# A layer of chunked attention and a mixture of experts on one Trainium2 core: all places of one attention block on the common time line, drawn anew

## What is computed

```python
x = x + layernorm(attention(layernorm(x)))        # 16 heads of 32, decayed linear attention in chunks of 128 tokens
x = x + layernorm(ffn(layernorm(x)))              # shared gated FFN (1408 wide) + top 2 of 8 experts (352 wide)

# attention, per head and chunk of 128 tokens, state S carried from chunk to chunk
inter  = (q * decay_q) @ S
intra  = ((q @ k.T) * decay_mask) @ v
S      = lam**128 * S + (k * decay_k).T @ v
out    = (inter + intra) @ w_out.T + b_out

# ffn, per token
shared = (silu(x @ gate.T) * (x @ up.T)) @ down.T
probs  = softmax(x @ router.T); top 2, renormalised
y      = sum over the 2 experts of weight * expert(x) + sigmoid(x @ shared_gate.T) * shared
```

## Time and profile before

| | us |
|---|---|
| median of 3 runs (lowest, highest) | 2009.27 (2005.46, 2009.52) |
| the profiled execution: span from first to last instruction | 2000.4 |
| its own time outside the span | not shown apart; the median of the runs is 8.9 above the span |
| TensorE busy | 1895.7 |
| VectorE, ScalarE, GpSimd busy | 1083.5, 844.6, 439.6 |
| mean granted TensorE clock | 0.985 |

### The profile page before, as it was taken

How to read it: one execution, slowest core, us unless ns; L and a number is a source line. 1 busy time by engine, 2 the same in 40 slices (tenths; PEclk the granted TensorE clock), 3 DMA queues, 4 the chain that set the end, 5 groups by cost and what they waited for, 6 DMA issues and landing times.

```text
span 2000.4 us, 27565 instructions
## 1 busy us (share of the span) xinstructions
PE 1895.7 (95%) x9880; PEld 1536.0 (77%) x9880; DVE 1083.5 (54%) x2590; ACT 844.6 (42%) x1718; POOL 439.6 (22%) x438
## 2 busy tenths in 40 slices
PE   7789999999999998999999999999999999999997
PEld 5567777777777776777777778778989888998875
DVE  4556665554554553464464454433656666666566
ACT  4334443333343332333344233123556656656554
POOL 2301001001001001001000100121455555555322
PEclk9889999999999998999999999999999999999998
DMA  8978566557367356446546456786788888888597
GB/s 304 373 258 310 184 246 250 198 187 258 122 234 259 126 173 243 177 163 239 205 174 224 171 181 240 243 325 236 236 253 241 247 247 240 255 250 251 130 283 198
DMA packets 140869, 456.84 MB, mean 228 GB/s; under 512 B 17200, under 2 KB 17344, under 8 KB 123968
## 3 DMA queue, kind: packets, MB, share of 16 engines
q1 hardware_dynamic: 90720, 251.70, 35.7%
q0 software_dynamic: 49584, 203.33, 33.0%
q10 hardware_dynamic: 432, 0.07, 0.0%
HBM read 332.99 MB, written 122.04 MB: 227 GB/s over the span
## 4 chain that ended last, share of the span: by engine, by line
PE 56%; DMA 5%; DVE 5%; ACT 2%; issue 1%; POOL 1%; SPq 1%; ACTq 0%; DVEq 0%
PE banks L796 16%; PE banks L798 16%; PE banks L797 16%; DMA moe_dn_raw<-w_dn,w_index 3%; PE banks L863 2%; PE banks L989 1%; DMA ffn_w_raw<-w_ffn 1%; PE banks L877 1%; PE banks L995 1%; PE banks L883 1%; PE banks L870 1%; DMA att_w_lo<-att_w_split 1%; PE banks L829 1%; ACT moe_dn_hi L1134 0%; DVE fin_stats L1535 0%
## 5 line engine op out<-in xcount | busy, mean ns | idle before, releaser
L796 PE MATMUL banks<-xT_hi,ffn_gate_up_hi_lo 128*128 128x512 f32 x704 | 296.7, 422 | 9.8 <-DMA xT_lo<-xt_scratch 3.3
L798 PE MATMUL banks<-xT_hi,ffn_gate_up_hi_lo 128*128 128x512 f32 x704 | 276.8, 393 | 0.0
L797 PE MATMUL banks<-xT_lo,ffn_gate_up_hi_lo 128*128 128x512 f32 x704 | 276.1, 392 | 0.0
L796 PE MATMUL banks<-moe_gu_hi,moe_xT_hi 128*128 128x352 f32 x568 | 196.5, 346 | 4.2 <-DVE moe_xT_lo L1515 4.1
L1067 ACT COPY q_one_head<-qT 32x128 f32<-32x128 f32 x512 | 151.2, 295 | 89.5 <-PE banks L863 84.0
L1508 DVE TENSOR_TENSOR moe_gu_lo<-moe_gu_raw,moe_gu_hi 128x704 fp32r<-128x704 f32 x156 | 136.0, 889 | 90.4 <-ACT moe_gu_hi L1128 85.7
L798 PE MATMUL banks<-moe_gu_hi,moe_xT_lo 128*128 128x352 f32 x568 | 183.4, 323 | 0.0
L797 PE MATMUL banks<-moe_gu_lo,moe_xT_hi 128*128 128x352 f32 x568 | 182.6, 321 | 0.0
L796 PEld LDWEIGHTS banks<-xT_hi,ffn_gate_up_hi_lo 128*128 128x128 f32 x704 | 133.1, 189 | 49.2 <-issue 10.2
L797 PEld LDWEIGHTS banks<-xT_lo,ffn_gate_up_hi_lo 128*128 128x128 f32 x704 | 133.2, 189 | 33.9 <-issue 8.9
L798 PEld LDWEIGHTS banks<-xT_hi,ffn_gate_up_hi_lo 128*128 128x128 f32 x704 | 132.9, 189 | 29.0
(11 more groups left out here) (315 smaller groups left out, 4157.6 us busy)
## 6 DMA issues: line engine op xcount, KB each, us to landing
ffn_gate_up_hi_lo<-ffn_gate_up_split SPq DMA_DIRECT2D x66, 1024.0 KB, 4.8
ffn_down_hi_lo<-ffn_down_split SPq DMA_DIRECT2D x66, 512.0 KB, 3.4
att_w_hi<-att_w_split SPq DMA_DIRECT2D x112, 256.0 KB, 4.0
att_w_lo<-att_w_split SPq DMA_DIRECT2D x112, 256.0 KB, 4.8
x_normed_by_expert<-x_normed POOLq DMA_DIRECT2D x26, 771.0 KB, 16.1
ffn_w_raw<-w_ffn SPq DMA_DIRECT2D x44, 384.0 KB, 6.0
ffn_gate_up_split<-ffn_gate_up_hi_lo SPq DMA_DIRECT2D x11, 1024.0 KB, 4.0
x_in<-x SPq DMA_DIRECT2D x32, 256.0 KB, 4.8
```

Of the source, the lines that this page charges most:

```text
L796: pe.matmul(out_ap, l_hi, r_hi, start=start, stop=False)
L797: pe.matmul(out_ap, l_hi, r_lo, start=False, stop=False)
L798: return pe.matmul(out_ap, l_lo, r_hi, start=False, stop=stop)
```

## The change

Every place in `PLACES` for an attention piece, load or store has a new number, and so have most in `OPENING` for QK to OUT. All kinds stay on the same engines and do the same work. As examples (`...` marks what is left out):

```diff
 PLACES = {
...
-    "wa": (7.25, 7.43, 7.61, 7.79, 10.52, 10.08, 12.52, 13.52, 14.17, 15.52, 16.52, 18.84, 23.22, 23.37, 23.52, 23.27,),
+    "wa": (7.45, 7.8, 8.11, 8.01, 10.94, 10.38, 11.08, 12.34, 14.6, 16.18, 18.65, 16.6, 25.8, 22.76, 21.02, 22.74,),
...
-    "x1o": (39.74, 41.3, 52.17, 54.37,),
+    "x1o": (46.37, 48.32, 57.11, 59.73,),
...
-    "SM4": (62.39,),
+    "SM4": (65.94,),
...
-    "sc": (59.43,),
+    "sc": (50.82,),
...
             elif kind == "S":
                 c, g = args
                 pe.wait_ge(a_piece, done("A", "Z", a, c, g))
+                if c == 0:
+                    pe.wait_ge(a_piece, done("A", "QK", a, G + g))
...
-            late = next(p for p in ORDER["V"] if p[0] in ("V", "KT"))
+            late = next(p for p in ORDER["V"] if p[0] in ("V", "KT", "S"))
```

More of the change, by code:

```diff
@@ L78 @@
 PLACES = {
[L79 to L83, removed]
-    "wa": (7.25, 7.43, 7.61, 7.79, 10.52, 10.08, 12.52, 13.52, 14.17, 15.52, 16.52, 18.84, 23.22, 23.37, 23.52, 23.27,),
-    "QK": (9.66, 11.07, 12.07, 13.22, 14.07, 15.07, 16.07, 16.78,),
-    "xr": (23.12, 24.37, 44.52, 44.74,),
-    "Z": (16.39, 18.62, 20.77, 21.47, 25.5, 26.5, 28.65, 29.05, 33.66, 33.97, 36.82, 37.52, 42.06, 43.54, 44.99, 45.76,),
@@ L99 @@
[L99 to L105, removed]
-    "SM4": (62.39,),
-    "CM": (61.75,),
-    "RK": (64.5,),
-    "sc": (59.43,),
-    "PG": (66.54,),
+    "xin": (-20.11, -13.36, -13.09, -10.59,),
+    "N1A": (-2.47,),
+    "N1B": (1.44,),
+    "N1": (2.58, 4.45, 5.36, 8.29,),
+    "T1": (4.9, 7.23, 8.34, 8.86,),
+    "wa": (7.45, 7.8, 8.11, 8.01, 10.94, 10.38, 11.08, 12.34, 14.6, 16.18, 18.65, 16.6, 25.8, 22.76, 21.02, 22.74,),
@@ new lines @@
+    "QK": (9.74, 10.42, 11.12, 12.9, 14.62, 15.27, 16.14, 17.29,),
+    "xr": (24.37, 31.32, 43.54, 44.04,),
+    "Z": (16.49, 19.13, 21.1, 22.12, 23.23, 23.53, 24.72, 24.75, 31.42, 34.52, 38.61, 38.77, 39.62, 41.87, 44.29, 45.63,),
+    "KT": (18.55, 25.13, 35.15, 42.61,),
+    "S": (18.34, 20.11, 22.41, 23.5, 27.51, 28.14, 30.65, 31.44, 33.99, 37.05, 39.39, 39.6, 44.56, 44.57, 47.4, 47.45,),
+    "V": (21.46, 22.04, 22.33, 23.82,),
+    "IP": (22.09, 24.7, 29.88, 32.57, 37.84, 40.73, 46.48, 48.78,),
@@ new lines @@
+    "ST": (24.9, 33.77, 41.37, 50.09,),
+    "OUT": (28.89, 35.29, 44.11, 50.35,),
+    "LO": (35.94, 51.93,),
+    "LN": (37.83, 52.9,),
+    "L": (39.32, 54.63,),
+    "LX": (41.16, 54.87,),
+    "x1o": (46.37, 48.32, 57.11, 59.73,),
+    "T2": (42.35, 45, 56.72, 57.2,),
+    "xto": (64.77,),
+    "R1": (58.8,),
+    "R2": (59.76,),
+    "SM1": (59.96,),
+    "SM2": (60.11,),
+    "SM3": (61.16,),
+    "SM4": (65.94,),
+    "CM": (61.93,),
+    "RK": (64.41,),
+    "sc": (50.82,),
+    "PG": (66.55,),
@@ L122 @@
     "T1": (4.47, 5.52, 6.47, 6.59,),
[7 rows of a table removed]
-    "OUT": (28.96, 35.39, 44.8, 50.87,),
[7 rows of a table added]
+    "OUT": (27.28, 33.29, 45.81, 51.24,),
 }
```

## The result

The changed kernel is slower: median 2065.47 us (2059.17 to 2069.38) against 2009.39 us (2005.46 to 2009.97) of the kernel before in the same comparison, a ratio of 1.028 with a 95% interval from 1.026 to 1.030. The profiled execution has a span of 2065.5 us against 2000.4, so 65.1 more; the medians differ by 56.1, as the profiled execution of before was a fast one (by the runs of the changed kernel a time is 1.8 us above its span, 2067.34 for 2065.5, so it took some 2002 us).

The account below looks back on a forecast made before the run. TensorE, busy 1895.7 of 2000.4 us, was taken as the bound. Terms 59.5 - 9.2 - 6.1 - 2.5 - 2.7 = +39.0 gave a span of 2039.4 and a median of 2048 us; range 1998 to 2068.

Parts of the forecast that it names:

- Part 1, the chain: Blocks 1 to 7, before OUT.a.0: scatter, store, x load delay wa.a.12; stall 6.0, clock 2.5; seven blocks cost 59.5 us.
- t = 503.1: Zero point of the chain's count in a block: the end of V.a.0 on TensorE.
- It lands 2.6 after its issue: Chain on GpSimd: the store x1o.(a-1).2, issued at 15.0 after t, lands 2.6 us later, at 17.6.
- OUT.a.0 waits for wa.a.12: Chain's end on TensorE: this load, issued at 18.5 after t, sets the stall of 6.0 us.
- The fourth rival: Full pile-up: stall 8.0 and clock 3 per block, half of the gains, +67, 2076 us; chance 0.11.
- The rest at nothing: xin, xr.a.1 to 3, wl loads and LX move some us with several us in hand; counted as nothing.
- Part 2, block 5: The 6.69 us wait for weight load wa.5.6 goes with its clock loss: -9.2 us.
- Part 3, KT: Blocks 1 to 7: a scores piece before KT.a.0 covers its 0.87 us wait for an eviction: -6.1 us.
- Part 4, the opening: Opening up to QK.1.0: -2.5 us, ends 0 and -5.3; the wait before GA.0 goes too, -2.7.
- Starts the fill some 8 us earlier: Opening: the zero fill starts some 8 us earlier, since S.0.0.0 stands three QK pieces of 2.8 us earlier.
- The cover itself: Opening: whatever TensorE saves before QK.1.0 it waits for there, behind zero fill and store x1o.0.0.
- The 2.69 us before GA.0: Opening: first FFN weights, raw.0, issue one QK piece earlier, so this wait goes: -2.7 us.

Follow-up runs that it names:

- the seventh experiment: Changed kernel with GpSimd's order as before and SP's four loads wa.a.12 to 15 ahead of the FFN load, xin and xr.a.0: 1984.34 us, 0.9906.
- the first experiment: Changed kernel with the scatter behind the stores x1o again on GpSimd, xto still behind the scatter: 2057.16 us, 1.0236.
- second: Changed kernel with SM4.a back behind CM.a on VectorE, so that the scatter starts earlier: 2054.97 us, 1.0231.
- fourth: Changed kernel with wa.a.12 ahead of xr.a.0 on SP, GpSimd as in the change: 2054.53 us, 1.0234.
- eighth: Changed kernel with only SP's order altered, the four loads wa.a.12 to 15 first, GpSimd as in the change: 2022.46 us, 1.0104.
- 9: Changed kernel with SP's four loads wa.a.12 to 15 first and xto ahead of the scatter, stores x1o still behind it: 1998.94 us, 0.9967.
- the eleventh experiment: Changed kernel with GpSimd's order as before, and the loads xr.0.0 and xr.0.1 issued as early as before: 2031.07 us, 1.014.
- the twelfth experiment: Changed kernel with SP's four loads wa.a.12 to 15 first, GpSimd's order as before and the old opening table: 1981.08 us, 0.9896.

## Why the prediction was right, and where it was not

The sign, the place and the range held: 2065 lies in 1998 to 2068 and in the forecast's own 2028 to 2068, the stalls stand in all seven blocks before OUT.a.0, end with att_w_lo, and drop the clock. The size was 17 us short, and the cause was only one part of it.

**Part 1, the chain, times.** With t = 503.1, 0.2 before the eviction of V.3.0 at 503.28, the scatter's last issue ends 14.9 later (517.99), by the prediction 14.7. Then comes the first step that failed: "It lands 2.6 after its issue". SP issued xr.3.0 at 526.73, 8.7 after the store, and the view of the stores by landing says the same:

```profile
out<-x POOLq DMA_DIRECT2D x2, 256.0 KB, 8.9
```

The store went into the stretch for which I had given the weight load 9.1 us (18.5 to 21.6 + 6.0), but took its own price from the median of all 32 stores. The trace of before already had a slow one. The landings of these stores there:

```profile
DMA to landing us min/median/max: 2.3/2.6/20.0
```

x1o.0.0, issued beside the zero fill, took 19.9. The load's own price was right: 9.0 us. TensorE would have been ready 22.8 after t, by the prediction 21.6. So the stall of block 3 is 10.8 instead of 6.0, and over seven blocks the mean is 9.8, above the upper end of 8.0. The clock fell as said, to between 0.69 and 0.83 in the 10 us behind the seven stalls, 0.76 in the mean. Its price was less: 45 to 50 matmuls start there instead of 56, an estimated 1.1 to 2.0 us of work lost each, and over all seven TensorE is busy for 1901.0 us where the seventh experiment, with the stalls nearly out, has 1892.4. That is 9 to 11 us and not 17.5.

**Part 1, the chain, as cause.** It is there, but cutting it gives 8 to 11 us, not the 68 to 85 that the first experiment expected (the first, second and fourth). The second step that failed, and the larger one, is "OUT.a.0 waits for wa.a.12": it waits for wa.a.12 to 15, and the prediction used the other three only as a surcharge on the landing of the first. wa.a.13, which no store holds up, by itself lands late enough for some 48 of the 68.3 us. So behind the chain, and of nearly the same length, lay a second cause: four loads on SP with a 1 MB FFN load among them, with the scatter and xto in the engines at the same time. "The rest at nothing" counted the wl loads by their own users; that one of them stands ahead of loads with 11 us to their user was left out. The seventh and eighth experiments show this cause: the order of the loads alone gives 36 us, with xto and the stores 75. The fourth rival names it ("2.8 MB of loads ahead on the same queue"), and its 2076 is nearer to the result than the forecast.

**Part 2, block 5.** Right: the 6.69 us are gone. No q or k projection of block 5 waits for more than half a microsecond, and the one such wait for a weight load behind the opening is 0.55 us in block 4.

**Part 3, KT.** The 6.1 us before KT went, but others came: over all blocks the transposes KT wait 9.2 us in the changed kernel, and 6.8 before. In their place TensorE waits for the eviction of the attention output. The new order of TensorE does not bring this by itself: with the same order of TensorE in blocks 1 to 7, KT waits 2.0 to 3.0 us in eight of the kernels above and 9.2 to 12.5 in four (the changed one and experiments 1, 4 and 9). What makes the difference stays open. The groups by line, after:

```profile
L859 PE MATMUL banks<-identity,kT 128*128 128x128 f32 x128 | 19.7, 276 | 9.2 <-DVE attT_lo L1367 4.8 <-ACT attT_hi L1076 1.7 <-DVE state L1373 1.3
```

**Part 4, the opening.** Wrong. QK.1.0 starts at 133.42, 8.0 later than before, where 2.5 were to be won. "Starts the fill some 8 us earlier" failed: the zero fill starts at 44.42 us, before it was 44.43, because VectorE's first part in S.0.0.0 comes late. GpSimd in time, its first fill after:

```profile
44.42 0.85 POOL L609 DMA_DIRECT2D ffn_out<-x_normed  x1 [26.02 <-DVE x_normed L1636]
```

VectorE makes what the fill waits for (L1636) right ahead of that part, at 43.59. So nothing made up for x1o.0.0 standing behind the whole fill: the store goes out at 113.99 instead of 97.02, and SP issues wa.1.0 at 128.57 instead of 118.89. The cover itself, by which savings ahead of QK.1.0 are worth nothing, was right, as the eleventh experiment shows. The 2.69 us before GA.0 went as said.

**The gains of the order** can be read where the stalls are out: the sum without Part 1 and without the opening's 2.5 is -9.2 - 6.1 - 2.7 = -18.0, and the twelfth experiment, which keeps the old opening, is 20.6 us faster than before (2001.67 to 1981.08). That the two are so near is in part luck: the twelfth still has 8.0 us of stalls before OUT, so its order gains more than was summed.

**Sum.** In the profiled execution +65.1 stand against +39.0. The span is TensorE's busy and idle time, so both can be split the same way:

| us | forecast | measured |
|---|---|---|
| stalls before OUT.a.0 | +42.0 | +68.3 |
| all other idle time of TensorE | -18.0 | -8.5 |
| busy time of TensorE (seven drops of the clock, less block 5's) | +15.0 | +5.3 |
| sum | +39.0 | +65.1 |

The forecast has the stalls 26 us too small, the gains in idle time 9.5 too large and the busy time 10 too large. That the time still fell into the range owes something to luck: the second and the third error offset each other, and the 8.9 us that the forecast added to get from a span to a median are some 0 for the changed kernel. Of the other idle time, the opening up to QK.1.0 has 7.7 us more instead of 2.5 less, and KT 2.4 more instead of 6.1 less. There are also gains that were not in the sum: small waits fell, such as that of the transposes of the normed rows, from 3.1 us to nothing:

```profile
L829 PE MATMUL banks<-identity,x_normed 128*128 128x128 f32 x128 | 19.5, 277 | 0.0
```

Not all of these are traced to a piece.

## What to carry to other kernels

A load's time to land belongs to the stretch in which it is in flight, not to its size: add up all bytes that all queues have in flight there, and order each queue by when its data is used. When a wait names a load, read in the code for which loads the instruction waits in all, and look up the landing of each. Where a chain of waits and a crowded stretch end at about the same time, removing the chain shows little; cut both before judging, and make a small table of combinations. An order that saves 1% on the engine that bounds the kernel can lose 3% by where loads and stores stand in two other queues.

## What the runs showed of the hardware

How long a transfer of 256 KB took to land went with what else was in flight. In the changed kernel the 112 low halves of the attention weights took 2.5 to 16.2 us:

```profile
DMA to landing us min/median/max: 2.5/4.3/16.2
```

Stores x1o of the same size took 2.6 us before, by the median, 19.9 beside the zero fill, and 8.7 and 9.2 in block 3 of the changed kernel, in flight with loads of another queue. In the crowded stretches some 410 GB/s were moved in all. The Trainium skill ("DMA: Bandwidth & Descriptors", Issuing engines are not separate DMA queues) says that all queues share the 16 engines and interleave; these rows agree. The loads that SP issued from 514.88 to 518.42, 11 times 256 KB, are by themselves an estimated 7.0 us at 410 GB/s. The Trainium skill's formula on that page ("DMA: Bandwidth & Descriptors", Anatomy of one DMA), from which the prediction took 2.6 us, is given there for DMAs issued from GpSimd; the median store before took as long. For the load, which SP issues, the prediction applied it as well and came to a landing near 21.7 (18.5 + 2.6 is 21.1); the load took 9.0 us, and in the crowded stretch the store took 8.7.
